# Attention inside a fused transformer stack: where the weighing of values stands between two scores, and where VectorE evacuates it

## What is computed

```python
q = x @ Wq.T                      # x: layer-normed, 4 batches of 512 tokens; 32 heads of 16
k, v = from(ctx)                  # 4 batches of 512 context tokens
q, k = rmsnorm(q), rmsnorm(k)     # over each head's 16
attn = softmax(q @ k.T * 16**-0.5)
out = attn @ v
x = x + tanh(g) * out
```

## Time and profile before

| | |
|---|---|
| median of 3 runs | 1234.15 us |
| profiled execution | 1236.31 us |
| its span in the trace | 1234.5 us |
| PE busy | 981.3 us (79%) |
| DVE busy | 718.4 us (58%) |
| ACT busy | 659.3 us (53%) |
| POOL busy | 538.6 us (44%) |
| mean granted TensorE clock | 0.921 of full speed |

### The profile page before, as it was taken

One profiled execution on the slowest core, in us unless ns is written; L12 is line 12 of the kernel. 1 busy time (PEld: TensorE's weight loads), 2 busy tenths in 40 slices (PEclk: granted clock), 3 DMA queues, 4 the chain that ended last, 5 costly groups with the idle time before them and its releaser, 6 DMA issues. The chain is left out here.

```text
span 1234.5 us, 27760 instructions
## 1 busy us (share of the span) xinstructions
PE 981.3 (79%) x9407; PEld 561.6 (45%) x9408; DVE 718.4 (58%) x1757; ACT 659.3 (53%) x1064; POOL 538.6 (44%) x467
## 2 busy tenths in 40 slices
PE   3799989967999697999999999643989789888200
PEld 1455655455777465677777777410222112111000
DVE  6676754587996365222232222153776887866784
ACT  3555545355454285444454444334778787999200
POOL 0232331255775364555565555342233443433535
PEclk9899999979999898999999999876999898999755
DMA  7343231499982786667776666476797768665110
GB/s 256 104 163 121 79 130 54 157 200 184 246 222 60 272 257 161 122 119 119 147 120 116 117 116 120 68 184 151 132 197 157 153 124 175 141 136 101 69 36 2
DMA packets 188066, 172.49 MB, mean 140 GB/s; under 512 B 141875, under 2 KB 143219, under 8 KB 187059
## 3 DMA queue, kind: packets, MB, share of 16 engines
q1 hardware_dynamic: 160368, 114.05, 36.6%
q0 software_dynamic: 26304, 56.98, 24.1%
q10 hardware_dynamic: 1298, 0.20, 0.1%
HBM read 81.12 MB, written 65.23 MB: 119 GB/s over the span
## 5 line engine op out<-in xcount | busy, mean ns | idle before, releaser
L1839 ACT ACTIVATE sb_atp<-ps_atpS 128x1024 f32<-128x1024 f32 x256 | 243.1, 1036 | 49.3 <-PE ps_atpS L1656 49.3
L1410 PEld LDWEIGHTS ps_shpH<-sb_roxT,sb_rowt 128*128 (+1 forms) x2844 | 170.1, 107 | 21.1 <-DVE sb_roxT L1277 1.8
L1410 PE MATMUL ps_shpH<-sb_roxT,sb_rowt 128*128 128x128 f16 (+1 forms) x2844 | 174.4, 221 | 1.7 <-DVE sb_roxT L1277 1.7
L1399 PE MATMUL ps_shpY<-sb_rowt,sb_rohhl 128*128 (+1 forms) x711 | 172.1, 388 | 2.5 <-DVE sb_rowt L1290 2.1
L1668 PE MATMUL ps_atpO<-sb_atp,sb_atv 128*17 128x512 f32 x1024 | 139.0, 615 | 31.0 <-ACT sb_atp L1839 20.8
L1034 POOL DMA_INDIRECT sb_roxg<-xn,sb_roentry x79 | 86.1, 1090 | 94.1 <-DMA sb_roentry<-list 71.1
L1133 ACT ACTIVATE sb_roh<-ps_shpH,sb_rob 128x128 f32<-128x128 f32 (+1 forms) x237 | 68.9, 362 | 103.8 <-PE ps_shpH L1410 101.4
L1399 PEld LDWEIGHTS ps_shpY<-sb_rowt,sb_rohhl 128*128 128x128 f16 (+1 forms) x711 | 67.6, 100 | 71.6 <-issue 8.6
L1656 PE MATMUL ps_atpS<-sb_atq,sb_atk 64*128 64x512 f16 x512 | 80.6, 395 | 23.1 <-DMA sb_atq<-qst 22.9
L1122 ACT ACTIVATE sb_roy<-ps_shpY,sb_roentry 128x512 f32<-128x512 f32 x79 | 54.2, 686 | 79.5 <-PE ps_shpY L1399 76.7
L1022 POOL DMA_INDIRECT list<-sb_shentry,sb_shposb x64 | 72.7, 1135 | 32.7 <-DVE sb_shposb L1205 17.3
(11 more groups left out here) (302 smaller groups left out, 1796.0 us busy)
## 6 DMA issues: line engine op xcount, KB each, us to landing
sb_rowt<-rw SPq DMA_DIRECT2D x15, 768.0 KB, 9.4
sb_rowt<-rw SPq DMA_DIRECT2D x15, 704.0 KB, 7.0
kst<-sb_kykp SPq DMA_DIRECT2D x16, 512.0 KB, 3.1
qst<-sb_quqp SPq DMA_DIRECT2D x16, 512.0 KB, 4.2
vst<-sb_kyvt SPq DMA_DIRECT2D x16, 272.0 KB
sb_atv<-vst SPq DMA_DIRECT2D x32, 136.0 KB, 3.7
sb_stage<-ctxT SPq DMA_DIRECT2D x4, 1024.0 KB, 7.1
sb_shxin<-x SPq DMA_DIRECT2D x16, 256.0 KB, 4.8
```

What stands on the lines that cost most here:

```text
L1399: last = e.matmul(pY[it.p][:, :], hhl[it.p][0:n, x, k * P:(k + 1) * P], weight(value, 2 * W1 + w + k * D, n, D), start=j == 0, stop=j == l ...
L1410: last = e.matmul(rpH[it.p][0:n, f * P:(f + 1) * P], weight(ex["up"], w + k * FF + f * P, P, n), rxT[it.p][:, x + k, :], start=j % (3 * KD ...
L1839: S.done(e.activation(pr[n % 6][:, :], pS[n % 3][:, :], ACT.Exp, scale=HD ** -0.5 / SA ** 2), "atexp")
```

## The change

On TensorE the loop goes by pairs `mm` (two per half beat) instead of by groups. A pair is: score 2m, the weighing of the pair two before (before: of the pair one before, after both scores), score 2m + 1; then, as before, at m = 2 the turn of the group before, at m = 3 the first half of a projection and at m = 0 the second half of the last one. A group's last weighing thus comes at m = 1 of the next group instead of m = 0, its first at its own m = 2 instead of m = 1.

On VectorE `evacuate` goes from the middle of the half beat to its end, behind projected, roots, scales, choose, spread2 and inner, and `scale` goes from the second place to behind normalise.

```diff
@@ tensor
-                for it in g_at(h, 0):
-                    for m in range(4):
-                        scores(it, 2 * m)
-                        scores(it, 2 * m + 1)
-                        if m > 0:
-                            weigh(it, m - 1)
-                        elif it.n > 0:
-                            weigh(it.back(1), 3)
-                        if m == 0 and it.n - 1 in started:
-                            project(started[it.n - 1], 6, 12)
-                        if m == 2 and it.n > 0:
-                            turn(it.back(1))
-                        if m == 3 and it.n in started:
-                            project(started[it.n], 0, 6)
-                if h == 2 * NG:
-                    weigh(It((NG - 1) // 2, 1), 3)
-                    turn(It((NG - 1) // 2, 1))
+                for mm in (2 * h, 2 * h + 1):
+                    now, old, done = (It(n // 8, n // 4 % 2) for n in (mm, mm - 2, mm - 6))
+                    if 0 <= mm < 4 * NG:
+                        scores(now, 2 * (mm % 4))
+                    if 2 <= mm < 4 * NG + 2:
+                        weigh(old, (mm - 2) % 4)
+                    if 0 <= mm < 4 * NG:
+                        scores(now, 2 * (mm % 4) + 1)
+                    if mm % 4 == 2 and 6 <= mm < 4 * NG + 6:
+                        turn(done)
+                    if mm % 4 == 3 and mm // 4 in started:
+                        project(started[mm // 4], 0, 6)
+                    if mm % 4 == 0 and mm // 4 - 1 in started:
+                        project(started[mm // 4 - 1], 6, 12)
@@ vector
                 for it in q_at(h, 2):
                     norm(it)
-                for it in n_at(h, 1):
-                    scale(it)
...
-                for it in g_at(h, 2):
-                    evacuate(it)
                 for it in q_at(h, 6, FIRST):
                     projected(it)
                 for it in g_at(h, 3):
                     normalise(it)
+                for it in n_at(h, 1):
+                    scale(it)
...
                 for it in c_at(h, 7):
                     inner(it)
+                for it in g_at(h, 2):
+                    evacuate(it)
```

## The result

The change makes the kernel slower: **1241.72 us** (median of 20 runs, 1237.75 to 1251.29) against 1236.26 us for the kernel before in the same rounds (1233.45 to 1240.39). The ratio is **1.0045**, interval 1.0031 to 1.0059, so some 5.5 us. I forecast 1233.0 us with a range of 1227.0 to 1239.5: the sign was wrong, and the time lies outside the range.

A forecast was written before the change was run, and what follows sets the result against it. ScalarE's exponentials were taken as the backbone, with TensorE bounding crowded groups and VectorE regions A and B. Gains of -8.3 and losses of +7.2 net -1.1 us, from 1234.15 to 1233.0 us, range 1227 to 1239.5.

The forecast's parts named there:

- first run: Groups 0 to 4: three periods' 0.16 us and half a microsecond at the edge, -1.0 us (bounds 0 and -2.6).
- turn 3 to 9: From the turn of group 3 to that of group 9: 54.8 us in place of 57.82, -3.0 us.
- region A: Turn 9 to turn 13: late copies and scale's move on VectorE make it longer, +2.2 us.
- region B: Turn 13 to turn 18: by the same terms, 52.9 us in place of 50.6, +2.3 us.
- region C: After turn 18, up to group 22: roots, inner and spread2 hold copies 19 and 20, +2.7 us (bounds 0 and +5).
- plain groups: Groups without a query projection, 9 from group 22 on: each loses its 0.32 us gap at the turn, -2.9 us.
- behind turn 31: The end: the inner sum now runs before the last copy instead of after it, -1.4 us (bounds 0 and -2.2).
- crowded period: Time of a group holding both halves of a projection: 9.71 us in place of 9.87, a gain of 0.16 each.
- part (c): Evacuation ending VectorE's half beat: turn-by-turn walk in which late copies cost +7.2 us over three regions of the attention.
- Slower: the turn stops TensorE and its clock falls: Rival: at turns 10, 14, 15 and 19 TensorE stands, its clock drops, pairs lose 1.21 us each; 1239.1 us, chance 0.25.
- Absorbed: Rival: stored scores and extra room before weighings swallow most of VectorE's lateness, 2.0 of 7.2 us stay; 1227.9 us, chance 0.25.
- Nothing changes: Rival: TensorE and VectorE are the bounds, so order may not matter; within 0.5 us of 1234.15, chance 0.10.

The follow-up runs named there:

- e9: The changed kernel with the weighing behind both scores of the pair instead of between them; ratio 1.0055 to the kernel before.
- e5: The changed kernel with scale back in its old place, second in VectorE's half beat; ratio 1.0041 to the kernel before.
- e3: The changed kernel with evacuate directly behind roots, ahead of scales, choose, spread2 and inner; ratio 0.9987 to the kernel before.
- e11: The kernel before with one Newton step in roots in place of three; ratio 0.9931 to the kernel before.
- e6: The changed kernel with evacuate back ahead of projected and scale back ahead of parts, leaving TensorE's new order alone; ratio 1.0135 to the kernel before.

## Why the prediction was wrong

The terms of the sum, in us, beside the changed profile's legs:

| | forecast | measured |
|---|---|---|
| first run | -1.0 | +0.3 |
| turn 3 to 9 | -3.0 | -2.0 |
| region A | +2.2 | **+4.3** |
| region B | +2.3 | **+3.8** |
| region C | +2.7 | **+4.9** |
| plain groups | -2.9 | -2.7 |
| behind turn 31 | -1.4 | -1.4 |
| sum | -1.1 | +7.2 |

Behind turn 31 it is 82.9 us (1238.3 - 1155.41) in place of 84.3 (1234.5 - 1150.21). But turn 31 itself came later: its copy had to wait 0.6 us longer for inner. From the last exponential's end to the end of the span it is 85.4 us in place of 86.2, so the end truly gained 0.8. The crowded period, forecast at 9.71 us, is 9.79 (858.48 to 868.27), so half the gain of 0.16 came. The changeover's price was not tested by itself: e9 keeps two changeovers in a plain pair, and its expectation was wrong to count one less.

**The step that failed** is part (c), the walk over regions A to C: its +7.2 measured +13.0. It failed not at the late turns but in what it counted behind them.

*The late turns were right.* The walk had 11.8 (968.14 and 0.1 on, less 956.44), 11.2 and 10.2 us from turns 9, 13 and 18 to the next turn. They took 12.21, 11.23 and 10.46, where before they took 7.66, 7.66 and 8.17. These three intervals alone are 10.4 of the 13.0 us. In each of them VectorE stood only for the turn at the start, 0.70 to 0.75 us, and then ran without a pause up to the copy: its queue set these turns. Turns 10, 14, 15 and 19, named in advance, wait 5.23, 4.30, 5.82 and 3.53 us; turn 11 waits 3.53 as well.

*The stretches behind them were not.* By the walk they would be 2.5 us shorter than before, all together; they are 2.6 us longer. Three terms were mis-sized:

- *Inner*, 2.24 us by its rows at the quiet end of the attention. Ahead of copy 11 it took 3.32 us (972.37 to 975.69), ahead of copy 15 4.17 (1018.72 to 1022.89), both beside work of GpSimd: 3.0 us more. Before the change it took 2.94 us behind copy 11, so the trace had a nearer row.
- *The second group behind a late turn*, 10.3 us. From turn 11 to turn 12 it took 11.44, and 11.33 before: the walk took off a microsecond that nothing in the change takes off.
- *Region C behind turn 19*: 10.64 us to turn 20 in place of 8.44. VectorE stood 1.21 us for turn 19, since scale no longer stood there to fill the time, line 1997 took 1.08 us in place of 0.22 beside a cast, and spread2 stood ahead of copy 20. Counted by turns, 18 to 21 took 28.3 us in place of 24.8; the other 1.4 us of region C's +4.9 come from where the leg is cut, since the first exponential of group 22 now stands 3.9 us ahead of turn 21 and no longer 5.3. Behind turn 19 the walk had added 0.7; it measured 2.6.

Together the three are some 6 us, where 5.1 are to be explained; smaller terms went the other way, scale's in A among them.

*Scale's move was priced by the right mechanism.* I wrote that GpSimd's casts and root, started later, would hold norm, 1.7 us each in A and B. The timeline of VectorE after, from copy 14 to copy 15, and that of GpSimd ahead of copies 11 and 15:

```profile
1008.70 0.69 DVE L1880 COPY sb_atoT<-ps_atpO 128x512 f32<-128x512 f32 x1
...
1015.56 0.15 DVE L1904 TENSOR_SCALAR sb_qurs<-sb_qurstd 128x1 f32<-128x1 f32 x1 [0.44 <-POOL sb_qurstd L1735]
...
1018.72 2.18 DVE L2007 TENSOR_SCALAR sb_laoh<-sb_lakey,sb_latop 128x64 f32<-128x64 f32 x1
...
1022.89 0.69 DVE L1880 COPY sb_atoT<-ps_atpO 128x512 f32<-128x512 f32 x1
```

```profile
966.84 2.41 POOL L1749 CAST sb_quqp<-sb_quqn 128x1024 f16<-128x1024 f32 x2 [3.48 <-DVE sb_quqn L1947]
969.22 0.98 POOL L1735 TENSOR_TENSOR sb_qurstd<-sb_quve,sb_mhalf 128x1 f32<-128x1 f32 x1
...
1016.17 3.02 POOL L1761 TENSOR_SCALAR sb_o<-sb_x,sb_laab 128x512 f32<-128x512 f32 x1
```

GpSimd's root ends at 970.20, and norm starts at 970.24; in B it is the same. Norm's wait shows as only 0.44 us because VectorE's operations ahead of it had become slower: lines 1987 and 1988, 0.21 and 0.74 us as a rule, took 0.87 and 1.59 beside the casts, 1.5 us more, once in A and once in B. The casts took 2.41 us, as against 2.42 before. So norm would have waited for the root all the same, and these 1.5 us moved nothing. With scale back (e5) copy 11 comes 11.68 us behind copy 10 in place of 12.90, and 1.21 of the 1.22 us lie ahead of norm. Copy 15 comes 11.79 us behind copy 14 in place of 14.19, and 2.0 of the 2.4 us lie ahead of norm. So the forecast 1.7 and 1.7 measured 1.2 and 2.0; behind norm, line 2007 took 2.18 us in B in place of 0.25, but what e5 has slower there makes up for most of it. In e5 regions A, B and C are shorter by 0.9, 2.5 and 1.2 us. The Trainium skill, SBUF — State Buffer, Who interferes with whom, says that a VectorE instruction with two SBUF inputs contends with a GpSimd instruction that reads SBUF, and that the shared port pair is an exclusive lock; the rows of lines 1987 and 1988, which have two such inputs, agree with it.

*The copy's place.* e3 gives 7.2 us in A to C for having scales, choose, spread2 and inner ahead of the copy; 5.8 of the 13.0 are left in e3, which has roots ahead of the copy and scale in its later place. A turn that is late delays its normalisation, that the next half of a projection, that the raw copy, and so the next copy's queue. The shares of scale's place (4.6 us by e5) and of the copy's place overlap and are not to be added.

*A part of "what bounds the kernel now" was wrong too:* "Here TensorE is the bound, and only 0.40 us per group is a matter of order." That fits up to turn 3, where e11 gains 0.2 us. Between turns 3 and 9 e11 gains 2.5 by VectorE's work alone.

**The rivals.** "Slower: the turn stops TensorE and its clock falls" has the right sign and nearly the time (1239.1; 1.0045 times 1234.15 is 1239.7), and its turns did stop TensorE. Its price is another matter. In stretches, after, of A, B and C (columns as in the earlier trace rows, with PEld, VectorE, ScalarE and GpSimd behind PE):

```profile
951.33:998.22 46.89, 37.38 (x235) 9.06 (x233) 36.26 (x104) 32.32 (x36) 18.84 (x18) 0.89 0.59 133
998.22:1052.53 54.31, 43.43 (x285) 10.34 (x285) 44.33 (x125) 39.20 (x43) 22.89 (x21) 0.91 0.66 141
1052.53:1076.88 24.35, 19.31 (x130) 4.29 (x130) 20.46 (x62) 18.67 (x22) 10.38 (x9) 0.86 0.47 115
```

and before:

```profile
956.44:999.02 42.58, 35.64 (x237) 8.11 (x233) 34.67 (x104) 31.41 (x35) 17.81 (x16) 0.92 0.70 141
999.02:1049.57 50.55, 43.17 (x288) 9.53 (x284) 41.82 (x125) 38.99 (x43) 22.61 (x21) 0.90 0.80 158
1049.57:1069.03 19.46, 16.54 (x128) 3.59 (x124) 17.46 (x57) 18.07 (x21) 8.68 (x7) 1.00 0.38 105
```

In B the mean clock is no lower than before (0.91 and 0.90), and 3.8 us are lost all the same. In C it fell from 1.00 to 0.86, and in A from 0.92 to 0.89, behind turns that had stood. The 10.4 us of the three late turns are none of the clock's, since VectorE hardly stood for TensorE there. The weighings of A to C that took over 1.2 us in place of 1.05 are 5 before and 7 after, in sum 3.3 and 5.0 us over: the weighings' slowness can account for at most 1.7 of the 13.0 us. e5 has 8 of them, 5.9 us over, and is shorter than the changed kernel. What the lower clock costs in the other matmuls, no run separates. "Absorbed" is refuted: nothing was swallowed. "Nothing changes" is refuted by the interval.

What is open: how the 5.8 us that e3 still loses in A to C divide between scale's place, roots ahead of the copy and the clock (of its 3.3 us in C, 1.6 lie between turns 18 and 21, the rest at the cut), and what a stretched operation costs where no wait covers it.

## What to carry to other kernels

A unit moved later on one engine makes its consumer wait later on the other, and the order of an in-order engine's queue decides what that costs: an instruction placed too early holds everything queued behind it (61.5 us of VectorE's time in e6), one placed too late holds the other engine (30.9 us of TensorE's in the changed kernel). Put it where its input arrives and no later: here behind projected or behind roots, where the new order cost nothing that could be told. Where two engines alternate on a chain, neither looks full, and a test that takes work from one of them, everything else unchanged, tells whether it is on the path; here 8.2 us less of VectorE's work gave 0.7% (at the price of rougher roots), and no order gave a gain that could be told from none. And take the duration of an operation from a row with the same neighbours on the other engines: inner at 2.24 us from a quiet place was 3.32 and 4.17 where it counted.

## What the runs showed of the hardware

A VectorE operation on one column (line 1987, 0.21 us) took 0.87 us, one of 64 columns (line 2007, 0.25 us) 2.18 us, with GpSimd casts, copies or a product running beside them, while the copy from PSUM (line 1880) kept 0.68 to 0.69 us in all 32 cases, 15 of them beside work of GpSimd. By its start and end no idle time shows: a busy VectorE may be one that stands. Summed over all of VectorE's instructions from the first exponential to turn 31, the time above the median of the same line and form is 13.7 us after the change, 7.1 before, 8.8 with scale back and 10.8 in e3. Where an operation stands in one engine's order thus goes with how long it and its neighbours take, and a sum of durations taken from another neighbourhood misses it. Not all of that time is lost: where the engine would have waited for the other anyway, as ahead of norm, it costs nothing.
